# The last pass of an attention kernel: the order and the place of its sixteen late output projections

## The chip, the cores and the metric

The kernel runs on one core of a Trainium2 chip. The metric is the device time of one execution in microseconds (us). Before the change it is 1885.85 us, the median of three runs (1885.11 to 1886.77). PE is the matrix engine, DVE the vector engine, ACT the scalar engine, POOL the GpSimd engine; SP issues all the transfers spoken of here.

## The reference, cut to what matters

```
x  = L0_attn_x                     # (4, 2048, 256) fp32
xn = layernorm(x)
q, k, v = low-rank projections of xn, 16 heads of 16; rotary embedding on half of q and k
att = softmax(causal(q @ k^T / 4))
y   = (att @ v), heads side by side, (4, 2048, 256)
out = x + y @ Wc + feed_forward(xn)
```

The change concerns `y @ Wc` for the last of the four batches, and the addition of it to the residual `x + feed_forward(xn)`.

## The kernel before, in words

A first stage (up to about 490 us of the span) makes the weights, Q, K, V and the residual R = x + feed_forward(xn), and stores them in DRAM. The second stage is attention. Its work is cut into 16 passes, called quads: 4 batches by 4 groups of 4 heads. The code is unrolled over them (`quads`, L1241). A pass has three strands, which share PE:

- **Entries** (115 a pass, `NE`): PE fills one of 3 PSUM banks `sm` (`fill`, L1693), DVE reads it. Most entries are the row maxima of the scores that the next pass needs. In the passes 4 to 15, four of them are projections of the batch before (`project`, L1670): 128 rows of `y` times `Wc`, two blocks of 128 contraction rows (`a`), each an fp32 128x256 product, which the profile shows as two matmuls; `add` on DVE (L1568) adds the bank to the residual. Entry e can be filled only when entry e-3 has been read (L1694).
- **Scores** (68 units a pass): PE fills one of 2 PSUM banks `st` (L1725), ACT takes the exponential into one of 8 `prob` buffers (L1529).
- **Sums** (36 steps a pass, `STEPS`): PE multiplies the exponentials by V and gathers 512 columns in `pv` (L1738). Steps 0 to 2 belong to chunk 0 of the batch, 3 to 9 to chunk 1, 10 to 20 to chunk 2, 21 to 35 to chunk 3 (`STEP_AT` = 0, 3, 10, 21). After a chunk's last step ACT copies `pv` to `Y` (`evac`, L1508). On the diagonal steps (18 to 20 and 33 to 35 among them) POOL first masks the exponentials (L1488).

PE and ACT run the same hand-written order (`TIMETABLE`, L1044, turned into `PLANS`). The last pass has no next pass, so its plan, `LAST` (L1090), drops the next pass's entries from step 13 on. In their place stand one entry for the last row maxima (`ROWS_LAST`, just ahead of step 14) and sixteen **late projections**, those of the last batch, chunks 12 to 15 with 4 blocks each. `BEHIND` (L1078) says behind which step of the sums each of them stands. Engines work through their queues in order: an entry that can't start holds up everything behind it on PE.

What a late projection needs:

- The sums of a pass are moved by SP to DRAM and to `Yc` (`move`, L1281), reloaded, inverted on DVE (`invert`), stored, and spread over partitions (`spread_inverse`, L1301); then POOL multiplies `Yc` by them (`normalise`, L1443, `normalise_late`, L1449) and raises `normed`. Of quad 15, chunks 12 and 13 come as the first half (its `normalise` stands ahead of POOL's masks for step 33, at n = 23), and chunk 14 by itself (`move_third`, `invert_third`, `normalise_late(1)`, at n = 33).
- Chunk 15 of the last head group is done in the tail, after the last step (`TURNED` and behind, L1792). What its late projections do is the *other* 12 heads: `project(..., others=True)`, where the second block has 64 contraction rows in place of 128. They need only the sums of quad 14 (`normalise_late(0)`, at n = 25).
- `add` waits for the residual of the chunk: `r_loaded >= 16 * g + 16` (L1575), and r_loaded counts the loads in the order of the chunks. Chunk 12's residual is loaded in the pass before. Those of chunks 13, 14 and 15 are loaded in SP's queue of the last pass (L1369 to L1372), behind the moves of the first half, the maxima's loads, the inverse's store and spread, and `store_out(11)`; chunk 13's load waits for that store to have landed, since it reuses its buffer:

```
1369  if quad >= TC:
1370      store_out(quad - TC)
1371      for g in range(quad - TC + 2, NCH if last else quad - TC + 3):
1372          load_r(g)
```

Order of the late projections before: behind steps 24 to 29 two each (chunk 12, chunk 13, chunk 15's other heads, four each), behind steps 29 to 32 one each (chunk 14); so three stand behind step 29. DVE runs `invert` for chunk 14's sums after the fourth of them. What follows step 32 is the same in both kernels: the sums of steps 33 to 35, the copy, two rounds of transposes, the last head group's projection, the last add and store.

Of the kernel before, what the change touches and what calls it, by code (L numbers as in the profile page):

```python
# [18 lines left out]
NCH = B * T // CH  # L19
SUB = CH // P  # L20
TC = T // CH
G = 4
NQ = B * H // G
QB = H // G
# [965 lines left out]
NE = len(SEQ)  # L990
# [10 lines left out]
def half_of(e):  # L1001

    return SEQ[e][1][0][0] % 2
# [9 lines left out]
LAG = 3  # L1013
# [21 lines left out]
UNITS, STEPS = len(UNIT), len(STEP)  # L1035
STEP_OF = [max(n for n in range(STEPS) if any(u == v for _, _, src in STEP[n][1] for v, _ in src)) for u in range(UNITS)]
UNITS_OF = [sorted({u for _, _, src in STEP[n][1] for u, _ in src}) for n in range(STEPS)]
STEP_AT = [min(n for n in range(STEPS) if STEP[n][0] == c) for c in range(TC)] + [STEPS]
# [34 lines left out]

ROWS_LAST, FIRST_TWO, LAST_BEFORE, THIRD = NE, NE + 1, NE + 1 + 2 * SUB, NE + 1 + 3 * SUB
TURNED, TURNED_BACK, LAST_OWN = NE + 1 + 4 * SUB, NE + 2 + 4 * SUB, NE + 3 + 4 * SUB
BEHIND = {STEP_AT[TC - 1] + 3 + i: (FIRST_TWO + 2 * i, FIRST_TWO + 2 * i + 1) for i in range(6)}  # L1078
for i in range(SUB):
    n = STEPS - LAG - SUB + i  # L1080
    BEHIND[n] = BEHIND.get(n, ()) + (THIRD + i,)


def late_block(e):

    n, s = divmod(e - FIRST_TWO, SUB)
    return NCH - TC + (0, 1, 3, 2)[n], s


LAST = []  # L1090
for x in FULL:
# [4 lines left out]
    if x[0] == "sums" and x[1] == 0:  # L1096
        LAST += [("entry", 0, e) for e in BEHIND.get(x[2], ())]
PLANS = [FULL, LAST]
# [34 lines left out]
def attention(nc, io, w, scr):  # L1133

    with ExitStack() as ctx:
# [3 lines left out]
        def sem(name):  # L1139
            return ctx.enter_context(nc.semaphore(name))  # L1140
# [48 lines left out]
        inverse_spread = sem("inverse_spread")  # L1189
# [30 lines left out]
        def unit_done(quad, number):  # L1220
            return quad * UNITS_RUN + (XAHEAD + number + 1 + ST)

        def normed_for(g):

            return QB * (g // TC) + QB - 1 + g % TC // 2 + (g == NCH - 2)

        def residual(g):

# [176 lines left out]
        def _(pool):  # L1405
# [37 lines left out]
            def normalise(quad, half):  # L1443

                pool.wait_ge(inverse_spread, 16 * G * (2 * quad + half + 1))
                y = Yc[quad // QB % 2][:, quad % QB // 2, WIDE * half:WIDE * (half + 1)]
                pool.tensor_tensor(out=y, in0=y, in1=spread[half][:, :], op=ALU.mult).then_inc(normed, 1)

            def normalise_late(n):  # L1449

                y = Yc[(NQ - 1) // QB % 2][:, (NQ - 1) % QB // 2, WIDE:2 * WIDE]
                if n == 0:
                    pool.wait_ge(inverse_spread, 16 * G * (2 * NQ - 1))
                    pool.tensor_tensor(out=y[0:G * DH, CH:], in0=y[0:G * DH, CH:], in1=spread[1][0:G * DH, CH:], op=ALU.mult)\
                        .then_inc(normed, 1)
                else:
                    pool.wait_ge(normed, NQ)
                    pool.wait_ge(inverse_spread, 16 * G * 2 * NQ)
                    pool.tensor_tensor(out=y[:, 0:CH], in0=y[:, 0:CH], in1=spread[1][:, 0:CH], op=ALU.mult).then_inc(normed, 1)
# [8 lines left out]

            def body(quad, slot, last):
                for n in range(STEPS):  # L1470
                    if last and n == STEP_AT[TC - 1] + SUB:
                        normalise_late(0)
                    if last and n == STEP_AT[TC - 1] + SUB * (TC - 1):
                        normalise_late(1)
                    if n == STEP_AT[TC - 1] and quad and quad % 2 == 0:
                        normalise(quad - 1, 1)
                    if n == STEP_AT[TC - 1] + (2 if last else SUB + 2) and quad % 2:
                        normalise(quad, 0)
                    if n == STEP_AT[TC - 1] and not last:
                        place_v(quad + 1, (slot + 1) % SLOTS)  # L1480
                    if n == STEP_AT[TC - 1] and quad + 2 < NQ:
                        difference_of_keys(quad + 2, (quad + 2) % SLOTS, ((quad + 2) // SLOTS + 1) * (16 * LOADS))
                    if not DIAGONAL[n]:
                        continue
                    for u in UNITS_OF[n]:
                        wait_apart(pool, spare, exp_done, unit_done(quad, NUMBERS[last][u]), pool_steps, 1)
                        for x, count in diagonal_blocks(quad, n, u):
                            pool.affine_select(out=x, in_=x, compare_op=ALU.is_ge, fill=0.0, base=0,  # L1488
                                               pattern=[[0, count], [1, P]], channel_multiplier=-1).then_inc(masked, 1)
# [53 lines left out]
        def _(dve):  # L1543
# [86 lines left out]
            def body(quad, slot, last):  # L1630
                for e in range(AHEAD, NE):
                    take(quad, slot, e, last)
                    if e == INVERT_LATE and quad:
                        invert(2 * quad - 1)
                if last:
                    split_rows(quad, slot, ROWS_LAST, NG - 1, NG)
                    invert(2 * quad)
                    for e in range(FIRST_TWO, TURNED):
                        add(quad, slot, e, *late_block(e))
                        if e == FIRST_TWO + SUB - 1:  # L1640
                            invert(2 * quad + 1)
                    return
                for e in range(AHEAD):
                    if e == INVERT_EARLY:
                        invert(2 * quad)
                    take(quad + 1, (slot + 1) % SLOTS, e, quad + 1 == NQ - 1)

            quads(body)
            quad, slot, g = NQ - 1, (NQ - 1) % SLOTS, NCH - 1
# [5 lines left out]
            for s in range(SUB):  # L1655
                own = yn[:, s, G * DH:].rearrange("p (h k) -> p h k", h=G)
                i = dve.tensor_tensor(out=own, in0=turned[:, s, :, 0:DH], in1=rec[:, s, :, None].to_broadcast([P, G, DH]), op=ALU.mult)
# [11 lines left out]
        def _(pe):  # L1669
            def project(dst, g, s, others=False):  # L1670

                pe.wait_ge(wc_loaded, 16)
                if g < 0:
                    for a in range(CC):
                        i = pe.matmul(dst[:, 0:C], lhsT=w["ident"][:, :], rhs=Wc[:, a, :], start=a == 0, stop=a == CC - 1)  # L1675
                    i.then_inc(sm_ready, 1)
                    return
                pe.wait_ge(normed, normed_for(g))
                t = CH * (g % TC) + P * s
                for a in range(CC):  # L1680
                    r = slice(0, G * DH if others and a == CC - 1 else P)
                    i = pe.matmul(dst[:, 0:C], lhsT=Yc[g // TC % 2][r, a, t:t + P], rhs=Wc[r, a, :], start=a == 0, stop=a == CC - 1)  # L1682
                i.then_inc(sm_ready, 1)
# [9 lines left out]
            def fill(quad, slot, e):  # L1693
                pe.wait_ge(sm_read, quad * NE + e + 1)  # L1694
                dst = sm[(slot * NE + e) % SM]
                if e > NE or e < NE and SEQ[e][0] == "project":
                    g, s = (quad - TC, SEQ[e][1]) if e < NE else late_block(e)
                    project(dst, g, s, e >= LAST_BEFORE and e < THIRD)
                    return
                if e == NE or SEQ[e][0] == "rows":  # L1700
                    n = NG - 1 if e == NE else SEQ[e][1]
                    if e == NE or n < NG - 1:
                        pe.wait_ge(m_ready, quad * NG + n + 1)
                    elif quad:
                        pe.wait_ge(m_ready, quad * NG)
                    pe.transpose(dst[:, 0:P], m[:, :], w["ident"][:, :]).then_inc(sm_ready, 1)
                    return
                half["last"] = half_of(e)
                for h, t, k, at in SEQ[e][1]:
                    r, width = slice(ROW * (h % 2), ROW * (h % 2) + KD), block_width(t, k)  # L1710
                    i = pe.matmul(dst[:, at:at + width], lhsT=Q[slot][r, h // 2, t * P:(t + 1) * P],  # L1711
                                  rhs=K[slot][r, h // 2, k * CH:k * CH + width], start=True, stop=True)
                i.then_inc(sm_ready, 1)
# [78 lines left out]
            dst = late_bank(TURNED)  # L1792
            pe.wait_ge(pv_read, NQ * TC + 1)
            for s in range(SUB):
                t = (TC - 1) * CH + s * P
                i = pe.transpose(dst[:, s * P:(s + 1) * P], Y[:, t:t + P], w["ident"][:, :])
            i.then_inc(sm_ready, 1)
            dst = late_bank(TURNED_BACK)
            for s in range(SUB):
                pe.wait_ge(yn_ready, s + 1)  # L1800
                i = pe.transpose(dst[:, s * P:(s + 1) * P], yn[:, s, :], w["ident"][:, :])
            i.then_inc(sm_ready, 1)
            pe.wait_ge(sm_read, quad * NE + SM + TURNED_BACK + 1)
            for k in range(2):
                dst = late_bank(LAST_OWN + k)
                for a in range(2):
                    s = 2 * k + a
                    i = pe.matmul(dst[:, a * C:(a + 1) * C], lhsT=ynT[:, s * P:(s + 1) * P], rhs=Wc[:, CC - 1, :], start=True, stop=True)
# [75 lines left out]
```

## Time and profile before

| | |
|---|---|
| median of the runs | 1885.85 us |
| the profiled execution | 1885.63 us |
| its span | 1883.9 us |
| granted TensorE clock, mean over the span | 0.982 |
| busy, share of the span | PE 97%, DVE 89%, ACT 84%, POOL 28% |

The profile is of one execution, whose own time is 1.7 us above its span. All places below are in microseconds from the start of the span. The last pass's part with which this document deals lies between 1822 and 1884. In a timeline, a row gives start, duration, engine, line and operation, out<-in, and how many instructions are merged in it; in brackets how long the engine had been idle, and what released it.

### The profile page before, as it was taken

To read this page: it belongs to the slowest core of one execution; us is meant where nothing else is said; L and a number is where in the kernel's file an instruction comes from. 1 tells how busy PE (TensorE), PEld (TensorE's weight loads), DVE (VectorE), ACT (ScalarE), POOL (GpSimd) and SP (SyncE) were. 2 spreads that over 40 slices of the span, in tenths; PEclk is the share of its full clock that TensorE was granted. 3 is DMA by queue.
4 is the path that set the end of the run, shared out by engine and by line. 5 is a ranking of instruction groups with operands and counts; after the bars stand their busy time and mean duration, and the time that the engine had idled before them with its cause. 6 is when DMAs were issued, how large, how long until landed. Compare 5 with 4: busy or idle time off the path is not lost.

```text
span 1883.9 us, 41858 instructions
## 1 busy us (share of the span) xinstructions
PE 1820.1 (97%) x13875; PEld 681.7 (36%) x13875; DVE 1670.1 (89%) x4759; ACT 1591.1 (84%) x1924; POOL 536.8 (28%) x647
## 2 busy tenths in 40 slices
PE   6999999999789999999999999999999999999998
PEld 3556555555322323233232323323232322323223
DVE  5899999999789999999999999999999999999961
ACT  4676676675169999999999999999999999999994
POOL 1121121121244141523414152441415144141220
PEclk8999999999769999999999999999999999999999
DMA  5232333335422314041431414143141414324112
GB/s 185 68 106 84 90 104 89 89 100 123 103 63 46 58 24 65 22 73 25 78 54 49 65 45 84 32 83 53 50 65 45 79 35 84 53 50 65 36 36 81
DMA packets 160324, 129.01 MB, mean 68 GB/s; under 512 B 95344, under 2 KB 144752, under 8 KB 159768
## 3 DMA queue, kind: packets, MB, share of 16 engines
q1 hardware_dynamic: 159064, 126.84, 31.2%
q8 instruction: 89, 1.46, 0.3%
q14 instruction: 83, 0.68, 0.1%
q10 hardware_dynamic: 1088, 0.03, 0.0%
HBM read 74.60 MB, written 42.98 MB: 62 GB/s over the span
## 4 chain that ended last, share of the span: by engine, by line
PE 43%; ACT 15%; issue 8%; DVE 5%; DMA 1%; POOL 1%; SPq 1%; DVEq 0%; ACTq 0%; POOLq 0%
PE pv L1749 16%; ACT prob L1529 13%; PE sm L1711 10%; PE st L1734 10%; PE sm L1682 3%; PE st L1721 2%; DVE sm L1610 2%; ACT excess L1522 1%; DVE sm L1598 1%; PE sm L1675 1%; DVE pm L1615 1%; DMA scratch_i<-inverse 1%; DVE pm L1598 1%; DVE pm L1610 1%; ACT Y L1512 0%
## 5 line engine op out<-in xcount | busy, mean ns | idle before, releaser
L1529 ACT ACTIVATE prob<-st 128x1024 f32<-128x1024 f32 x1088 | 1048.1, 1028 | 53.6 <-PE st L1734 43.6
L1749 PE MATMUL pv<-prob,V 128*32 128x512 f32 (+3 forms) x5120 | 586.4, 539 | 0.3 <-ACT Y L1512 0.2
L1598 DVE CUSTOM_DVE_ANT_0 sm<-sm,mask 128x256 f32<-128x256 f32 (+3 forms) x1024 | 473.4, 520 | 32.0 <-PE sm L1711 27.3
L1711 PE MATMUL sm<-K,Q 48*128 48x512 f16 (+3 forms) x2112 | 479.7, 348 | 13.2 <-DVE pm L1598 5.5
L1734 PE MATMUL st<-Q,K 50*128 50x512 f16 (+3 forms) x2560 | 478.5, 352 | 9.8 <-ACT prob L1529 6.0
L1615 DVE TENSOR_REDUCE pm<-sm 128x1 f32<-128x512 f32 x640 | 412.0, 683 | 39.9 <-PE sm L1711 36.6
L1488 POOL TENSOR_SCALAR_AFFINE_SELECT prob<-prob 128x256 f32<-128x256 f32 (+1 forms) x448 | 191.4, 442 | 869.6 <-ACT prob L1529 860.5
L1610 DVE CUSTOM_DVE_ANT_0 sm<-sm,excess 128x512 f32<-128x512 f32 x448 | 301.2, 711 | 17.9 <-PE sm L1711 17.3
L1711 PEld LDWEIGHTS sm<-K,Q 48*128 48x128 f16 x2112 | 151.9, 95 | 327.9 <-DVE pm L1610 115.0
L1734 PEld LDWEIGHTS st<-Q,K 50*128 50x128 f16 x2560 | 125.7, 93 | 363.1 <-ACT prob L1529 265.2
L1522 ACT ACTIVATE excess<-st 128x1024 f32<-128x1024 f32 x218 | 220.4, 1024 | 8.7 <-DVE pm L1615 5.1
L1749 PEld LDWEIGHTS pv<-prob,V 128*32 128x32 f32 x5120 | 107.4, 108 | 172.8 <-issue 152.6
L1598 DVE DVE_READ_ACCUMULATOR2_ANT pm<- 128x1 f32 x1024 | 143.5, 140 | 0.1
L831 ACT ACTIVATE g<-bank 128x512 f32<-128x512 f32 x128 | 76.7, 599 | 55.8 <-PE bank L904 55.8
L722 DVE SCALAR_TENSOR_TENSOR gl<-g,wlnw,gh 128x512 f16<-128x512 f32 x128 | 106.9, 873 | 10.0 <-ACT gh L834 9.4
L866 PE MATMUL bank<-wWP,gh 128*128 128x256 f16 x512 | 113.6, 273 | 0.0
L866 PE MATMUL bank<-wWP,gl 128*128 128x256 f16 x512 | 113.5, 273 | 0.0
L1721 PE MATMUL st<-DK,Q 48*128 48x512 f16 x448 | 97.9, 389 | 7.1 <-POOL DK L1441 5.9
L659 POOL TENSOR_TENSOR frs<-fve,wmhalf 128x4 f32<-128x4 f32 x16 | 16.2, 1009 | 286.6 <-DVE fve L789 286.6
L834 ACT ACTIVATE gh<-g,wlnw 128x512 f16<-128x512 f32 x128 | 93.6, 731 | 0.0
L836 ACT ACTIVATE g<-g 128x512 f32<-128x512 f32 x128 | 81.5, 637 | 0.0
L904 PE MATMUL bank<-wxh,wWF 128*128 128x512 f16 x256 | 77.9, 386 | 0.1
(201 smaller groups left out, 1899.4 us busy)
## 6 DMA issues: line engine op xcount, KB each, us to landing
Q<-scratch_q SPq DMA_DIRECT2D x102, 128.0 KB, 4.3
K<-scratch_k SPq DMA_DIRECT2D x102, 128.0 KB, 7.1
x<-in_x SPq DMA_DIRECT2D x16, 512.0 KB, 4.4
scratch_v<-Rt SPq DMA_DIRECT2D x64, 128.0 KB, 2.0
scratch_r<-Rt SPq DMA_DIRECT2D x16, 512.0 KB, 3.2
V_raw<-scratch_v SPq DMA_DIRECT2D x16, 512.0 KB, 10.1
Yc<-Y SPq DMA_DIRECT2D x124, 64.0 KB
spread<-scratch_i SPq DMA_DIRECT2D x124, 64.0 KB, 2.2
```

The lines of the kernel that those rows point to most:

```text
L722: dve.scalar_tensor_tensor(out=gl[:, hc, :], in0=g[:, hc, 0, :], scalar=w["lnw"][:, hc:hc + 1], in1=gh[:, hc, :], op0=ALU.mult, op1=ALU.su ...
L866: pe.matmul(bank[s][:, 0:C], lhsT=x[:, hc, s * P:(s + 1) * P], rhs=w["WP"][:, hc, :], start=hc + k == 0, stop=hc + k == HC)
L1488: pool.affine_select(out=x, in_=x, compare_op=ALU.is_ge, fill=0.0, base=0, pattern=[[0, count], [1, P]], channel_multiplier=-1).then_inc(m ...
L1522: act.activation(excess[((slot + ahead) % SLOTS * NX + k) % EXCESSES][:, :, :], st[number % ST][:, :, :], ACT.Relu)\
L1529: act.activation(prob_of(quad, k)[:, :, :], st[number % ST][:, :, :], ACT.Exp).then_inc(exp_done, 1)
L1598: i = dve.tensor_tensor_reduce(x, x, mask[:, CH - block_width(t, k):], 1.0, -3e38, ALU.add, ALU.max, best(h, t, k))
L1610: dve.tensor_tensor_reduce(bank[:, :], bank[:, :], excess[(slot * NX + r) % EXCESSES][:, h % 2, :], 1.0, -3e38, ALU.add, ALU.max, best(h, ...
L1615: dve.tensor_reduce(out=best(h, t, k), in_=bank[:, :], axis=AX.X, op=ALU.max).then_inc(sm_read, 1)
L1711: i = pe.matmul(dst[:, at:at + width], lhsT=Q[slot][r, h // 2, t * P:(t + 1) * P], rhs=K[slot][r, h // 2, k * CH:k * CH + width], start=Tr ...
L1721: i = pe.matmul(st[number % ST][:, g, :], lhsT=Q[slot][rows[g], h // 2, t * P:(t + 1) * P], rhs=DK[slot][rows[g], h // 2, :], start=True, ...
L1734: i = pe.matmul(st[number % ST][:, a, at:at + width], lhsT=K[slot][r, hp, j * P:(j + 1) * P], rhs=Q[slot][r, hp, (c + 1) * CH - width:(c + ...
L1749: i = pe.matmul(pv[2 * DH * h:2 * DH * (h + 1), CH - width:CH], lhsT=V[quad % VSLOTS][:, j, h, :], rhs=prob_of(quad, u)[:, h % 2, at:at + ...
```

## The change

The late projections get another order (chunk 15's other heads first, then chunks 12, 13 and 14) and other places: behind steps 16, 18, 20 and 21; behind 21, 22, 23, 24; behind 25 to 28; behind 29 to 32. Only step 21 has two. On POOL `normalise_late(0)` moves from n = 25 to n = 10 and waits for the spread of quad 14 alone, and the counts of `normed` follow. DVE inverts chunk 14's sums after the sixth late entry in place of the fourth. The loads on SP stay as they are.

```diff
@@ -1073,18 +1073,16 @@
-ROWS_LAST, FIRST_TWO, LAST_BEFORE, THIRD = NE, NE + 1, NE + 1 + 2 * SUB, NE + 1 + 3 * SUB
+ROWS_LAST, LAST_BEFORE, FIRST_TWO, THIRD = NE, NE + 1, NE + 1 + SUB, NE + 1 + 3 * SUB
 TURNED, TURNED_BACK, LAST_OWN = NE + 1 + 4 * SUB, NE + 2 + 4 * SUB, NE + 3 + 4 * SUB
-BEHIND = {STEP_AT[TC - 1] + 3 + i: (FIRST_TWO + 2 * i, FIRST_TWO + 2 * i + 1) for i in range(6)}
-for i in range(SUB):
-    n = STEPS - LAG - SUB + i
-    BEHIND[n] = BEHIND.get(n, ()) + (THIRD + i,)
+LATE_AT = (16, 18, 20, 21) + (21, 22, 23, 24, 25, 26, 27, 28) + (29, 30, 31, 32)
+BEHIND = {n: [LAST_BEFORE + i for i, at in enumerate(LATE_AT) if at == n] for n in LATE_AT}
 
 def late_block(e):
-    n, s = divmod(e - FIRST_TWO, SUB)
-    return NCH - TC + (0, 1, 3, 2)[n], s
+    n, s = divmod(e - LAST_BEFORE, SUB)
+    return NCH - TC + (3, 0, 1, 2)[n], s
@@ -1222,7 +1220,9 @@
         def normed_for(g):
-            return QB * (g // TC) + QB - 1 + g % TC // 2 + (g == NCH - 2)
+            if g >= NCH - TC:
+                return NQ + (0, 0, 1, -1)[g % TC]
+            return QB * (g // TC) + QB - 1 + g % TC // 2
@@ -1450,7 +1450,7 @@
                 if n == 0:
-                    pool.wait_ge(inverse_spread, 16 * G * (2 * NQ - 1))
+                    pool.wait_ge(inverse_spread, 16 * G * (2 * NQ - 2))
@@ -1468,7 +1468,7 @@
                 for n in range(STEPS):
-                    if last and n == STEP_AT[TC - 1] + SUB:
+                    if last and n == STEP_AT[TC - 2]:
                         normalise_late(0)
@@ -1635,9 +1635,9 @@
                     invert(2 * quad)
-                    for e in range(FIRST_TWO, TURNED):
+                    for e in range(LAST_BEFORE, TURNED):
                         add(quad, slot, e, *late_block(e))
-                        if e == FIRST_TWO + SUB - 1:
+                        if e == FIRST_TWO + 1:
                             invert(2 * quad + 1)
@@ -1695,7 +1695,7 @@
-                    project(dst, g, s, e >= LAST_BEFORE and e < THIRD)
+                    project(dst, g, s, e >= LAST_BEFORE and e < FIRST_TWO)
```

## Rows read from the trace of the kernel before

**Rows 1.** Windows of the last pass: stretch, length, busy by engine, clock, DMA share, GB/s

```profile
1832.00:1837.00 5.00, 3.85 (x44) 1.19 (x42) 0.00 (x0) 4.90 (x7) 3.58 (x2) 1.00 0.54 164
1837.00:1842.00 5.00, 4.61 (x34) 0.93 (x34) 0.00 (x0) 4.97 (x6) 0.00 (x0) 1.00 0.92 297
...
1862.00:1867.00 5.00, 5.00 (x26) 2.22 (x24) 1.26 (x3) 1.93 (x2) 0.00 (x0) 1.00 0.01 3
```

**Rows 2.** Timeline of ACT, ahead of the late projections

```profile
1834.08 8.49 ACT L1529 ACTIVATE prob<-st 128x1024 f32<-128x1024 f32 x9
```

**Rows 3.** Timeline of PE: the sums of step 18 and of step 21

```profile
1830.05 1.06 PE L1749 MATMUL pv<-prob,V 128*32 128x512 f32 x8
...
1834.23 1.06 PE L1749 MATMUL pv<-prob,V 128*32 128x512 f32 x8 [0.18 <-ACT Y L1512]
```

**Rows 4.** Timeline of PE, 1854 to 1871: scores, and the sums of steps 28, 30, 31, 32

```profile
1854.40 0.61 PE L1734 MATMUL st<-Q,K 50*128 50x512 f16 x4
1855.97 0.39 PE L1734 MATMUL st<-Q,K 50*128 50x512 f16 x2 [0.96 <-ACT prob L1529]
1856.29 1.06 PE L1749 MATMUL pv<-prob,V 128*32 128x512 f32 x8
...
1865.12 1.07 PE L1749 MATMUL pv<-prob,V 128*32 128x512 f32 x8
...
1867.50 1.06 PE L1749 MATMUL pv<-prob,V 128*32 128x512 f32 x8
...
1870.10 1.06 PE L1749 MATMUL pv<-prob,V 128*32 128x512 f32 x8
```

**Rows 5.** The chain that ended last: two late projections (chunk 12, chunk 15), sums, one

```profile
1842.17 1.92 PE sm L1682 x8
...
1857.36 2.51 PE sm L1682 x8
...
1865.19 0.99 PE pv L1749 x8
1866.18 1.06 PE sm L1682 x4
```

**Rows 6.** Timeline of SP: a store, the residuals' loads, and the next move

```profile
1831.48 0.42 SPq L1344 DMA_DIRECT2D out<-Rt  x1
1834.53 0.40 SPq L1340 DMA_DIRECT2D Rt<-scratch_r  x1
1834.97 1.06 SPq L1340 DMA_DIRECT2D V<-scratch_r  x2
1836.07 1.24 SPq L1317 DMA_DIRECT2D scratch_l<-Y  x4
```

**Rows 7.** Line 1340 in the last pass: the residuals of chunks 13, 14, 15

```profile
DMA to landing us min/median/max: 4.0/5.0/6.5
```

**Rows 8.** Timeline of DVE: the first late add

```profile
1843.27 0.42 DVE L1576 TENSOR_TENSOR Rt<-Rt,sm 128x256 f32<-128x256 f32 x1 [19.88 <-PE sm L1682]
```

**Rows 9.** Timeline of POOL: normalising chunks 12 and 13, and chunk 14

```profile
1833.21 2.37 POOL L1447 TENSOR_TENSOR Yc<-Yc,spread 128x1024 f32<-128x1024 f32 x1 [2.77 <-DMA spread<-scratch_i]
...
1853.04 1.27 POOL L1459 TENSOR_TENSOR Yc<-Yc,spread 128x512 f32<-128x512 f32 x1 [16.25 <-DMA spread<-scratch_i]
```

**Rows 10.** Windows of PE alone at low clock: stretch, length, busy, clock, DMA share, GB/s

```profile
39.00:42.00 3.00, 1.82 (x3) 0.57 0.00 0
42.00:46.00 4.00, 3.94 (x11) 0.50 0.06 6
46.00:50.00 4.00, 4.00 (x19) 0.97 0.37 127
490.00:494.00 4.00, 0.00 (x0) 0.50 0.48 105
548.00:552.00 4.00, 4.00 (x38) 1.00 0.02 6
```

**Rows 11.** Timeline of PE: the first matmul of the attention stage

```profile
494.82 0.34 PE L1754 MATMUL pv<-ident 128*128 128x1 f32 x1 [6.17 <-PEq L539]
```

## The prediction

> **What bounds the kernel now.** I read the page's busy shares first (PE 97%), and then only the last pass, since nothing else is touched. Windows of five microseconds split that pass [rows 1]. Up to 1842 ACT is the full engine (4.90 and 4.97 of 5), and PE has gaps (3.85 and 4.61 busy): ACT takes nine exponentials without a pause [rows 2], and DVE, with nothing to do for 19.88 us, waits for the first late projection [rows 8]. From 1842 on the late projections sit on PE, which is then full while ACT falls to 1.93 of 5. So one part of the pass wastes PE and the next wastes ACT. What sets the end is PE's queue; the tail behind it is the same in both kernels. The most that an even spread can give back is PE's idle time ahead of 1842, of which these ten microseconds hold 1.54 (1.15 and 0.39), and a little from 1827 to 1832.
>
> **What the early places need.** Three conditions hold the first entries; I take them in turn.
> *Normalising.* Chunk 15's other heads need quad 14's sums only, a pass old, so POOL can multiply at n = 10. The nearest row, the same columns on twice the partitions, takes 1.27 us [rows 9]; I take that, and at nothing on the path, since POOL is busy for 28% of the span and its next work is the masks of step 18. If that cover were gone it would put those masks, and step 18, off by at most the 1.27. Chunk 12, now behind step 21, needs the multiply that starts at 1833.21 and takes 2.37, so it is ready at 1835.6 [rows 9].
> *Banks.* Of 3 `sm` banks one holds the last maxima, read long before. So the entries behind steps 16, 18 and 20 can be filled, and the fourth (the first behind step 21) waits until DVE has added the first.
> *The residual.* That first add is now chunk 15's, and waits for chunk 15's residual, where before it was chunk 12's, loaded a pass earlier. SP stores chunk 11 at 1831.48, waits for it, issues chunk 13's load at 1834.53 and the other two from 1834.97; the last is issued at about 1835.5 [rows 6]. Landing takes 4.0, 5.0 and 6.5 us [rows 7]; the queue is shared, so I give the longest to the last: 1835.5 + 6.5 = **1842.0**. Nothing that SP waits for ahead of it is moved by the change, so this time stays.
>
> **Where the stall is.** Before, step 21 starts at 1834.23 [rows 3] and its sums take 0.99 [rows 5], so the place of the fourth entry is reached at 1835.2. Three entries of chunk 15 now stand ahead of it: two of these took 2.51, so 1.25 each [rows 5], 3.8 in all. PE's waits for ACT take up part; if all, PE gets there at 1835.2, if none, at 1839.0. I take 1838, because ACT is already the slower engine there and only about 1 us of gaps lies between step 16 and step 21. PE then waits for the landing (1842.0), DVE's add (0.42 [rows 8]) and a hand-over of under 0.1: it goes on at **1842.5** after 4.5 us idle (3.5 to 7.3 by the bounds). Everything queued behind waits too: three score units, so ACT, which runs dry one exponential after the other, and step 22.
>
> **The sum, from 1842.5 to step 30.** Behind it PE is the bound to the end, so its pieces are added up at the prices of the rows.
> - The fourth entry, 1.25; the fifth, a full one, 1.06 [rows 5].
> - Three score units and then sums: 1854.40 to 1856.29 is 1.89, of which 0.96 is PE waiting for an exponential because there are 2 score banks [rows 4]. The same happens here.
> - A step of sums, one projection and two units takes 1870.10 - 1867.50 = 2.60 [rows 4]. From step 22 to step 27 there are five: 13.0.
> - Step 27 to 28 has three units: 0.99 + 1.06 + 1.89 = 3.94.
> - Step 28 to 29 has one unit: 1867.50 - 1865.12 = 2.38. Step 29 to 30: 2.60.
> Together 26.12, so step 30 starts at 1868.6. Before it starts at 1865.12 [rows 4]: **+3.5 us**. In this lies the dearer spread: two full ones together cost 1.92, alone 2.12, so four split pairs cost 0.8. From step 30 on both orders are the same, and nothing is added.
> What else moves costs nothing. Chunk 14's inverse is asked for after the sixth entry's add, about 1849.3, against 1847.9 before; its multiply was at 1853.04 [rows 9], so it comes at about 1854.5 and is wanted behind step 29, at 1866. The add itself (0.42 of DVE) is in time everywhere. `move_third` on SP needs chunk 2's copy, which comes some 2 us later (about 1836.3) than now but only 0.3 behind the queue's own 1836.07 [rows 6]. The stores of chunks 12 and 13 move to about 1854 and 1867, far from the last.
>
> **The clock.** A wait of 4.5 us does more than pass time. At 490 to 494 PE is idle and the granted clock is 0.50 [rows 10]; the first matmul after that ended 6.17 us of idleness [rows 11], so the fall to the 1.2 GHz level came within the first microseconds of it. Between 39 and 50 the clock is low for 0.43 / 0.5 of 3.00, all of 4.00 and 0.03 / 0.5 of 4.00, that is 2.6 + 4.0 + 0.2 = 6.8 us, and rises while PE works without a pause; the other stretch at the low level is the whole way from 490 to 548, on work full of short gaps [rows 10]. With no idle time like this in any pass of before, no row shows a gap of exactly this length. I price the fall by the nearest stretch, 6.8 us, since the work after the stall is dense: half of it is lost, 3.4, less about 0.4 because the 0.96 us wait for the exponential shrinks when PE is slow: **+3.0 us**. Bounds: 0 (no fall), and 26 / 2 = 13 if it stays low up to step 30.
> The Trainium skill, "TensorE: Matmul & The Clock Gate", section "HAM oscillation — how this bites in real kernels", describes just this: a wait for a transfer between bursts of matmuls sends the array back to half rate, and the next burst starts slow. By that rule the sum is 3.5 + 3.0; by a reading in which only the idle time counts it is 3.5.
>
> Sum: 1885.63 (the profiled execution's own time) + 6.5 = 1892.1. The median of the runs is 0.2 above that execution, so I forecast 1892.3.
>
> **The rivals.**
> A. *Stall and fallen clock*, as above: 1892.3. For it: the landing follows from SP's queue alone, and the clock's fall at 490. Chance 0.66.
> B. *Stall, and the clock holds.* The waits of up to 1 us in the last pass leave it at 1.00 [rows 1, 4]; 4.5 us might fall so that it holds too. 1885.85 + 3.5 = 1889.3. Chance 0.20; it straddles the bound of 0.2% (1889.6), so 0.13 of it is no change and 0.07 slower.
> C. *The clock stays low*, as it did from 490 to 548, because the steps' waits for ACT keep it there: 1885.85 + 3.5 + 13 = 1902. Against: PE leaves few gaps once it is the bound. Chance 0.05.
> D. *The residual is not late, and the gaps are filled.* Its place is the fourth entry; it decides if chunk 15's load has landed by 1838. Then PE goes on at 1838.0 (chunk 12's multiply, done at 1835.6, would be the next condition, and is met), and 1838.0 + 26.1 puts step 30 at 1864.1, 1.0 us earlier: 1884.8. With no ACT waits left at all it would be 1883; even that is within 0.2%. Against it: three loads of 512 KB behind a store, with DMA at 0.92 busy up to 1842 [rows 1]. Chance 0.09, of which 0.02 faster than 0.2%.
>
> **How the numbers follow.** 0.2% is 3.8 us, about what can be told from no change here. Slower: 0.66 + 0.07 + 0.05 = 0.78; same: 0.13 + 0.07 = 0.20; faster 0.02. The range starts at 1888.6, which takes in B, and ends at 1896.5, where the low stretch is about 14 us in place of 6.8. C and D are outside.
>
> **What would show it.** Right: in the new trace one idle time of PE of 4 to 5 us, ended by DVE's add to V (chunk 15's residual), ahead of the first of the two entries behind step 21; the first late add at about 1842.0, released by a DMA; ACT idle for some 6 us around 1839 to 1845; a granted clock below 1.00 in a window behind 1838; step 30 between 1868 and 1873; the tail unchanged in length. The step on the residual is wrong if the first late add starts well before 1841; the step on the clock if the windows keep 1.00. A time below 1885 would refute the argument as a whole.

## The result, and the profile after

| | before | changed |
|---|---|---|
| median | 1885.88 us (5 runs) | 1894.61 us (5 runs, 1893.09 to 1896.75) |
| ratio | | 1.0047, 95% interval 1.0036 to 1.0058 |
| profiled execution, span | 1885.63, 1883.9 | 1893.09, 1891.3 |
| mean granted clock | 0.982 | 0.980 |

The change costs 8.7 us. The ratios here and below leave out two executions of later rounds that ran far outside all others, one of the kernel before (5870 us) and one of the later start with its waits used (2012 us). The profiled execution of the changed kernel reached the last pass 1.1 us earlier than that of before (DVE splits the last maxima at 1821.74, and at 1822.85 before), a difference that stands already at the first sums of the attention (546.3, and 547.9 before), which the change doesn't touch. So 1.1 is to be added to its places before they are set against those of before; the span's 7.4 us more are 8.5 from there on.

PE's timeline of the changed kernel, from the sums of step 19 to step 30 (columns as in [rows 4]):

```profile
1832.78 1.50 PE L1749 MATMUL pv<-prob,V 128*32 128x384 f32 x24
...
1835.90 1.06 PE L1749 MATMUL pv<-prob,V 128*32 128x512 f32 x8
1841.35 4.38 PE L1682 MATMUL sm<-Wc,Yc 128*128 128x256 f32 x8 [4.38 <-DVE V L1576]
1845.65 1.03 PE L1734 MATMUL st<-Q,K 50*128 50x512 f16 x4
1847.44 0.61 PE L1734 MATMUL st<-Q,K 50*128 50x512 f16 x2 [0.75 <-ACT prob L1529]
1847.98 1.93 PE L1749 MATMUL pv<-prob,V 128*32 128x512 f32 x8
1849.84 2.08 PE L1682 MATMUL sm<-Wc,Yc 128*128 128x256 f32 x4
1851.85 1.03 PE L1734 MATMUL st<-Q,K 50*128 50x512 f16 x4
1852.82 1.51 PE L1749 MATMUL pv<-prob,V 128*32 128x512 f32 x8
1854.25 1.13 PE L1682 MATMUL sm<-Wc,Yc 128*128 128x256 f32 x4
...
1872.56 1.07 PE L1749 MATMUL pv<-prob,V 128*32 128x512 f32 x8
```

Two things are to be seen. PE is idle for 4.38 us behind step 21, and DVE's add to `V` (where chunk 15's residual lies) lets it go on. And for the next 12 us its work takes nearly twice as long: sums 1.93 for 1.06, one projection 2.08 for 1.13 (in [rows 4, 5], as after 1854 here, they have their old durations).

DVE's and ACT's timelines of the same stretch say who waits for what, and SP's and its landing when the data came:

```profile
1840.87 1.08 DVE L1576 TENSOR_TENSOR V<-V,sm 128x256 f32<-128x256 f32 x3 [18.59 <-DMA V<-scratch_r]
...
1852.30 0.35 DVE L1566 RECIPROCAL inverse<-sums 128x32 f32<-128x32 f32 x1
```

```profile
1846.36 2.85 ACT L1529 ACTIVATE prob<-st 128x1024 f32<-128x1024 f32 x3 [8.57 <-PE st L1734]
```

```profile
1833.89 1.06 SPq L1340 DMA_DIRECT2D V<-scratch_r  x2
```

```profile
DMA to landing us min/median/max: 4.0/5.0/6.3
```

The first late add was released by PE before [rows 8]; now a transfer releases it, and three adds follow at once, since three banks stood full. SP's loads are where they were [rows 6, 7], but for the 1.1 us. ACT stands for 8.57 us.

Windows of the changed kernel over the stall and behind it (columns as in [rows 1]):

```profile
1836.00:1840.00 4.00, 0.97 (x8) 0.06 (x8) 0.00 (x0) 1.80 (x2) 0.00 (x0) 1.00 1.07 356
1840.00:1844.00 4.00, 2.65 (x5) 1.35 (x6) 1.33 (x4) 0.00 (x0) 0.00 (x0) 0.51 0.05 7
1844.00:1848.00 4.00, 3.25 (x13) 1.08 (x13) 0.60 (x2) 1.64 (x2) 0.00 (x0) 0.50 0.00 0
1848.00:1852.00 4.00, 4.00 (x16) 1.49 (x16) 0.04 (x1) 1.22 (x2) 0.00 (x0) 0.50 0.01 4
1852.00:1856.00 4.00, 4.00 (x24) 1.14 (x24) 1.06 (x3) 2.13 (x3) 0.00 (x0) 0.78 0.09 21
1856.00:1860.00 4.00, 4.00 (x27) 1.47 (x22) 0.42 (x1) 3.34 (x4) 1.27 (x1) 1.00 0.23 64
```

The granted clock is at the 1.2 GHz level for 3.9 + 4.0 + 4.0 + 1.8 = 13.7 us, from just after 1840, while PE still stood, to about 1853.8.

**Where the 8.5 us are.** PE goes on at 1841.35 and starts step 30 at 1872.56: 31.2 us, where the prediction's pieces sum to 26.1 at full clock. So 5.1 us are the clock's, and 3.4 the stall's and the split pairs'. Of the 13.7 us at the low level 1.2 passed while PE still stood and cost nothing; over the other 12.4 the loss is 0.4 of the time, not half, since the work took 1.8 times as long (1.93 for 1.06) and the wait for an exponential was shorter. Behind step 30 the two traces run alike: from there to the tail's first transposes it is 10.83 us in both (1865.12 to 1875.95, and 1872.56 to 1883.39).

### The profile page after: what moved, and what is told of

It reads as the page before. It is cut to its first block, busy times and chain, and to the rows that moved or that the text cites. A ratio compares the mean times of both kernels' runs of the same rounds, so it can differ in the third digit from the quotient of the medians.

```text
span 1891.3 us, 41858 instructions
## 1 busy us (share of the span) xinstructions
PE 1826.5 (97%) x13875; PEld 685.3 (36%) x13875; DVE 1670.7 (88%) x4759; ACT 1591.4 (84%) x1924; POOL 535.9 (28%) x647
## 4 chain that ended last, share of the span: by engine, by line
PE 46%; ACT 12%; issue 7%; DVE 5%; DMA 2%; SPq 1%; POOL 1%; DVEq 0%; ACTq 0%; POOLq 0%
PE pv L1749 18%; PE st L1734 11%; PE sm L1711 11%; ACT prob L1529 10%; PE sm L1682 3%; PE st L1721 2%; DVE sm L1610 2%; DVE sm L1598 1%; ACT excess L1522 1%; PE sm L1675 1%; DVE pm L1615 1%; DMA scratch_i<-inverse 1%; DVE pm L1598 1%; DVE pm L1610 1%; PE sm L1706 0%
## 5 line engine op out<-in xcount | busy, mean ns | idle before, releaser
L1682 PE MATMUL sm<-Wc,Yc 128*128 128x256 f32 (+1 forms) x256 | 76.0, 420 | 4.8 <-DVE V L1576 4.4
```

## The experiments

Theory 1 is the prediction's: chunk 15's residual lands late, the fourth late entry waits, and the wait brings the clock down. Theory 2: the order or the spread costs by itself. Theory 3: chunk 12's multiply is the next thing to be late. Ratios are against the kernel before, on the same chip and in the same rounds (its medians there: 1885.90, 1886.42 and 1886.25 us). Each row stands for 3 to 11 executions, of which one has a profile.

| run | median us | ratio, 95% interval |
|---|---|---|
| early residual | 1884.81 | 0.9995 (0.9986 to 1.0004) |
| before, with the early load | 1886.38 | 1.0002 (0.9992 to 1.0011) |
| first of the three loads | 1887.46 | 1.0007 (0.9997 to 1.0016) |
| later start | 1884.26 | 0.9994 (0.9985 to 1.0003) |
| order alone | 1886.04 | 0.9997 (0.9988 to 1.0006) |
| stall filled, 20 matmuls | 1890.19 | 1.0023 (1.0013 to 1.0032) |
| stall filled, 15 | 1894.04 | 1.0039 (1.0027 to 1.0051) |
| stall filled, 10 | 1894.55 | 1.0041 (1.0026 to 1.0057) |
| changed kernel again | 1894.92 | 1.0045 (1.0030 to 1.0060) |
| before, two waits used | 1884.43 | 0.9989 (0.9980 to 0.9998) |
| early residual, waits used | 1883.27 | 0.9983 (0.9974 to 0.9992) |
| later start, waits used | 1883.85 | 0.9990 (0.9981 to 0.9999) |

### Taking the wait away: an earlier load

```diff
                     spread_inverse(quad - 1, 1)
+                if last:
+                    load_r(NCH - 1)
                 move(quad, 0)
...
-                    for g in range(quad - TC + 2, NCH if last else quad - TC + 3):
+                    for g in range(quad - TC + 2, NCH - 1 if last else quad - TC + 3):
```

Chunk 15's load and its add get a semaphore of their own, `last_loaded`.

> The changed kernel, but chunk 15's residual is loaded earlier in SP's queue, with a semaphore of its own. Theory 1 (the residual's late landing makes the stall, and the stall makes the clock fall): no PE idle time above 1 us in the last pass, clock 1.00 throughout, 1884.9 us, within 1 us. Theory 2 (the order itself costs: split pairs, fewer gaps, the clock falling on denser mixed work): the time stays above 1889. Theory 3 (chunk 12's multiply becomes the next wait): PE stalls some 1 to 2 us ahead of the fifth late entry, 1886 to 1887.

Measured: 1884.81 us. PE's timeline around the place of the stall:

```profile
1835.68 1.06 PE L1755 MATMUL pv<-prob,V 128*32 128x512 f32 x8
1836.67 2.39 PE L1688 MATMUL sm<-Wc,Yc 128*128 128x256 f32 x8
1838.99 0.61 PE L1740 MATMUL st<-Q,K 50*128 50x512 f16 x4
1840.57 0.39 PE L1740 MATMUL st<-Q,K 50*128 50x512 f16 x2 [0.96 <-ACT prob L1532]
...
1862.78 1.06 PE L1755 MATMUL pv<-prob,V 128*32 128x512 f32 x8
```

Step 21's sums go straight over into the fourth and fifth entries; the longest wait is the known 0.96 for an exponential. From the fourth entry to step 30 it is 26.1 us, and the granted clock is 1.00 in all of 1830 to 1880. The whole loss is gone with one load, so neither the order nor the spread nor chunk 12's multiply makes it. The control, on the kernel before:

> Control: the kernel before with the same earlier load of chunk 15's residual. No theory has a gain for it, since no add of before waits for a residual: 1885.9 us, within 0.7 us. If it gained, the gain of the first run would be the load's and not the order's.

1886.38 us, no gain: the load matters only where something waits for it.

### A dose of the landing

```diff
+                    if last:
+                        sp.wait_ge(out_stored, 16 * (NCH - TC))
+                        load_r(NCH - 1)
-                    for g in range(quad - TC + 2, NCH if last else quad - TC + 3):
+                    for g in range(quad - TC + 2, NCH - 1 if last else quad - TC + 3):
```

> The changed kernel, but chunk 15's residual is the first of the three loads behind the store, not the last; nothing else of the queue moves. It is issued at about 1834.5 and lands after 4.0 us, at 1838.5, the add is done at 1838.95: PE waits about 1 us in place of 4.4. Theory 1: the stall follows the landing; 1884.8 + 1.0 = 1885.8 us if the clock holds as in the waits of 0.96, some 4 more if it falls. Were the wait for anything but the landing, it would stay at 4.4 us.

PE's, then DVE's timeline of it:

```profile
1838.02 2.38 PE L1689 MATMUL sm<-Wc,Yc 128*128 128x256 f32 x8 [1.04 <-DVE V L1583]
```

```profile
1837.54 1.08 DVE L1583 TENSOR_TENSOR V<-V,sm 128x256 f32<-128x256 f32 x3 [15.25 <-DMA V<-scratch_r]
```

The wait follows the landing: 1.04 us in this execution. The profiled execution took 1884.63 us with the clock at 1.00; the median, 1887.46, is 1.7 above what I expected. The ten executions spread from 1884.63 to 1889.74, and only one has a profile. That in some of them the clock fell would fit, but isn't shown.

### The place and the order apart

```diff
-LATE_AT = (16, 18, 20, 21) + (21, 22, 23, 24, 25, 26, 27, 28) + (29, 30, 31, 32)
+LATE_AT = (18, 20, 22, 23) + (24, 24, 25, 25, 26, 26, 27, 28) + (29, 30, 31, 32)
```

> The changed kernel with chunk 15's four entries behind steps 18, 20, 22 and 23, then two behind each of 24, 25 and 26, and one behind each of 27 to 32; the loads are untouched. Theory 1: the fourth entry is reached at about 1841.7, the wait for the residual shrinks to under 1 us, the clock holds, and PE's gaps up to 1842 are partly filled: 1884.9 us, within 1 us. Theory 2 (order): most of the loss stays, above 1889.

1884.26 us: the four entries stand two steps later (and six of the other twelve in pairs again), and the loss is gone without touching a load. DVE's first add waits for the transfer as in the changed kernel, but PE has work until then. DVE's, then PE's timeline of it, up to the fourth entry:

```profile
1841.75 1.08 DVE L1576 TENSOR_TENSOR V<-V,sm 128x256 f32<-128x256 f32 x3 [18.69 <-DMA V<-scratch_r]
```

```profile
1841.40 1.06 PE L1749 MATMUL pv<-prob,V 128*32 128x512 f32 x8
1842.40 1.11 PE L1682 MATMUL sm<-Wc,Yc 128*128 128x256 f32 x3
```

With the order alone, all in the old places (24, 24, 25, 25, and so on):

> The changed kernel's order (chunk 15's other heads first, then 12, 13, 14) in the places of before: two behind each of steps 24 to 28, three behind 29, one each behind 30 to 32. Theory 1 (only the place against the landing of the residual matters): the first add comes after 1843, when the residual is there, so nothing waits: 1885.9 us, within 0.7. Theory 2 (the order costs by itself): above 1887.

1886.04 us. The order costs nothing, and gains nothing.

### The clock apart from the stall

The stall's length is fixed by the landing, so work put into it doesn't prolong it while it ends by then; it only keeps PE busy. (The twenty matmuls below end just with it: DVE's first add starts at 1841.26 and PE goes on at 1841.74.)

```diff
+            def keep_busy(quad, slot, count):
+                number = XAHEAD + NUMBERS[True][45]
+                pe.wait_ge(exp_done, quad * UNITS_RUN + number + 1)
+                for _ in range(count):
+                    pe.matmul(st[number % ST][:, 0, :], lhsT=K[slot][0:KD + 2, 0, 0:P], rhs=Q[slot][0:KD + 2, 0, 0:CH],
+                              start=True, stop=True)
```

It is called ahead of the fourth late entry.

> The changed kernel with 20 matmuls of 128x512 put in ahead of the fourth late entry, into a score bank that is overwritten next; their results are not used. They fill the stall with work and remove nothing of it. Theory 1: PE still goes on only when the residual has landed (about 4.4 us lost to filler), but the clock stays at 1.00, so only the stall's part is left: 1885.9 + 3.5 = 1889.4 us, and the difference to the changed kernel, about 5 us, is the clock's price. Theory 2 (the clock falls for another reason, or costs little): the time stays at 1894 or is above it.

PE's timeline:

```profile
1836.26 1.07 PE L1756 MATMUL pv<-prob,V 128*32 128x512 f32 x8
1837.30 4.49 PE L1742 MATMUL st<-Q,K 50*128 50x512 f16 x20
1841.74 2.39 PE L1682 MATMUL sm<-Wc,Yc 128*128 128x256 f32 x8
...
1867.84 1.06 PE L1756 MATMUL pv<-prob,V 128*32 128x512 f32 x8
```

and its windows:

```profile
1836.00:1842.00 6.00, 6.00 (x31) 2.22 (x30) 0.74 (x3) 1.94 (x2) 0.00 (x0) 1.00 0.80 255
1842.00:1850.00 8.00, 7.03 (x40) 2.76 (x40) 1.87 (x6) 4.36 (x5) 0.00 (x0) 1.00 0.03 4
```

With 4.4 us of useless work added and nothing removed the kernel is 4.4 us *faster* than the changed one (1890.19 against 1894.61). The clock stays at 1.00, and from the fourth entry to step 30 it takes 1867.84 - 1841.74 = 26.10 us. This splits the loss by medians: 4.3 us for the stall and the pairs (1890.19 - 1885.90; 3.5 were expected), 4.4 for the clock. One of the ten executions took 1894.11; it has no profile.

Ten and fifteen of the matmuls in place of twenty:

> As the kernel with 20 filler matmuls, but with 10: about 2.2 us of the stall stay idle. The stall's length is the same, so only the clock can differ. If a wait of this length brings the clock down as 4.4 us did: about 1894. If it does not: 1890, as with 20. I expect it to fall in some executions, with a median of 1891 and a wider spread than with 20.

> 15 filler matmuls in the stall, between 10 (2.12 us left idle, the clock fell) and 20 (0.0 idle, it held). About 1.1 us stay idle, as much as the waits of 0.96 which leave the clock at 1.00 everywhere. If the length of a single wait decides: the clock holds, 1890.2 us. If it falls here too, something else in that stretch (the filler's kind of work, the sparse steps ahead) is needed beside the wait: about 1894.

Ten leave 2.12 us idle, fifteen 0.98, as PE's timelines have it:

```profile
1843.45 4.37 PE L1682 MATMUL sm<-Wc,Yc 128*128 128x256 f32 x8 [2.12 <-DVE V L1576]
```

```profile
1841.57 2.39 PE L1682 MATMUL sm<-Wc,Yc 128*128 128x256 f32 x8 [0.98 <-DVE V L1576]
```

With ten, all four executions took 1893.24 to 1895.39 us, and the profiled one shows 4.37 us for two projections, the low level. I had expected 1891. Its windows have the fall within the wait:

```profile
1838.00:1842.00 4.00, 3.33 (x19) 0.98 (x18) 0.00 (x0) 1.86 (x2) 0.00 (x0) 1.00 1.08 352
1842.00:1846.00 4.00, 2.55 (x5) 1.25 (x6) 1.23 (x4) 0.00 (x0) 0.00 (x0) 0.58 0.07 11
```

PE stands from 1841.33, and by the 0.58 the low level begins at about 1842.6, 1.3 us later. In the changed kernel it began 3.1 us after PE fell idle (1836.97 to 1840.1). So a wait of 2.12 us behind ten filler matmuls is enough.

With fifteen, two of six took 1888.86 and 1889.80 and four 1893.55 to 1896.55. The 1889.80 is the profiled one: 2.39, full clock. The gap of 4 us between the two groups is that between the kernels with 20 and with 10, so I read it as the clock falling in four of six. That is read from times alone: in the one profile, with 0.98 us idle, the clock held, and how long PE waited in the four others isn't recorded. So it isn't shown that a wait of 0.98 us can bring the clock down. The waits of 0.96 behind steps 21 and 27 leave it at 1.00 in the traces of the early residual and of the kernels with 15 and 20. Whether the filler's narrow operands (50 rows) or the sparse steps ahead play a part was not tried. The Trainium skill, "TensorE: Matmul & The Clock Gate", section "HAM oscillation — how this bites in real kernels", tells of waits for transfers of several microseconds that bring the clock down; the changed kernel agrees with it, 4.38 us and then 13.7 at the low level. A fall in a wait of 2.12 us it does not tell of.

The changed kernel once more:

> The changed kernel once more, for a second look at its clock: the stall is 4.4 us again; the time at the low level may differ from 13.65 us, since the five runs of it spread over 3.7 us. 1894.6 us.

1894.92 us; windows of its profiled execution (1896.35 us):

```profile
1840.00:1844.00 4.00, 0.00 (x0) 0.00 (x0) 0.05 (x1) 0.57 (x1) 0.00 (x0) 1.00 0.81 248
1844.00:1848.00 4.00, 3.58 (x7) 2.10 (x8) 1.45 (x4) 0.00 (x0) 0.00 (x0) 0.51 0.02 2
1848.00:1852.00 4.00, 3.25 (x16) 0.52 (x15) 0.42 (x1) 2.56 (x3) 0.00 (x0) 0.50 0.01 4
1852.00:1856.00 4.00, 4.00 (x24) 1.45 (x16) 0.68 (x2) 1.16 (x2) 0.00 (x0) 0.71 0.00 0
```

Here the low level lasts 3.9 + 4.0 + 2.3 = 10.2 us in place of 13.7. It began 4.3 us after PE fell idle, and 3.1 us in the first profile; that is 1.2 of the 3.5 us, and what makes the rest isn't shown. Both profiles have the whole stall, 4.4 and 4.7 us. From the fourth entry to step 30 it takes 1874.49 - 1844.42 = 30.07 us, so the clock costs 4.0 us here and 5.1 in the first profile. The execution is the longer one all the same: the last maxima are split 2.8 us later (1824.51, for 1821.74), and the last projection runs at the low level.

### Using PE's waits

The gains so far are within the noise. Two waits of PE in the kernel before can be filled without any of the change: the 0.96 us behind step 27 [rows 4], and the one ahead of the last step's sums, which wait for the last unit's exponential and mask.

```diff
+for e, n, u in ((FIRST_TWO + 7, STEP_AT[TC - 1] + 6, 59), (THIRD + SUB - 1, STEPS - LAG - 1, 67)):
+    BEHIND[n] = tuple(k for k in BEHIND[n] if k != e)
+AMID = {59: (FIRST_TWO + 7,), 67: (THIRD + SUB - 1,)}
...
+    if x[0] == "scores":
+        LAST += [("entry", 0, e) for e in AMID.get(x[2], ())]
```

> The kernel before, with two of its late projections moved into PE's waits: the second of those behind step 27 goes between the second and the third score unit behind it (PE waits 0.96 there), and the last one goes behind the last score unit, so that its exponential and its mask run beside it (PE has some 0.6 idle ahead of the last step of sums). If PE is the bound to the end: 1885.9 - 1.5 = 1884.4 us. If the tail is bound elsewhere: 1885.9.

1884.43 us, 0.9989 (0.9980 to 0.9998): as expected, and with an interval below 1. The same with the early load, and with the later start (a string names the score unit behind which an entry stands):

```diff
+LATE_AT = (16, "39", 18, 20) + ("46", 22, 23, 24, 25, 26, 27, "59") + (28, 29, 31, "67")
...
+LATE_AT = (18, 20, "46", 23) + (23, 24, 24, 25, 25, 26, 27, "59") + (28, 29, 31, "67")
```

> The early load of the residual with the late projections from step 16 on, each put where PE waits: behind step 16, after the first unit behind 17, behind 18 and 20, after the second unit behind 21, behind 22 to 27, after the second unit behind 27, behind 28, 29 and 31, and after the last unit. Theory 1: no stall, clock 1.00, and against the early load alone (1884.8) the two waits of 0.96, half of one of 0.43 and the 0.6 ahead of the last step are filled: 1882.1 us. If PE's waits come back elsewhere: 1884 to 1885.

> No load is moved. Chunk 15's entries behind steps 18 and 20, after the second unit behind 21 and behind 23; the rest one or two a step, with one in the wait behind step 27 and one behind the last unit. Theory 1: the wait for the residual is under 1 us and the clock holds; against the kernel with the later start (1884.3) the wait of 0.96 and the 0.6 ahead of the last step go: 1882.8 us, as good as with the early load (1883.3).

1883.27 us (0.9983, 0.9974 to 0.9992) and 1883.85 us (0.9990, 0.9981 to 0.9999). Both beat both kernels; they can't be told from each other, nor clear of noise from the kernel before with its two waits used (1884.43). Against the kernel before of their own rounds they gain 3.2 and 2.4 us; of this the two waits give 2.0 by themselves (1886.42 - 1884.43), and the earlier places about 1, which is what the first experiment had given (1885.90 - 1884.81 = 1.1, itself within the noise). The first was expected at 1882.1 and came at 1883.27, the second at 1882.8 and came at 1883.85. PE's waits behind step 27 in the first are gone:

```profile
1855.44 0.60 PE L1743 MATMUL st<-Q,K 50*128 50x512 f16 x4
1855.97 1.13 PE L1691 MATMUL sm<-Wc,Yc 128*128 128x256 f32 x4
1857.04 0.39 PE L1743 MATMUL st<-Q,K 50*128 50x512 f16 x2
```

## Why the prediction was right, and where it was off

- **The residual, not the multiply or the bank count alone.** Right. The load was to land at 1842.0 and PE to go on at 1842.5; it went on at 1841.35, which with the 1.1 us of the earlier start is 1842.45. The idle time was to be 4.5 us and is 4.38. ACT was to be idle for some 6 us and stood for 8.57: the two projections behind the stall, which stand ahead of its next scores on PE, took 4.38 us in place of 2.39.
- **The sum from there to step 30.** Right: 26.12 was predicted, and both kernels in which the clock held show 26.1 (early residual, stall filled). That includes the dearer single projections.
- **What was taken at nothing.** POOL's multiply ran at n = 10 in POOL's idle time. Chunk 14's inverse came at 1852.30, which in the places of before is 1853.4, not 1849.3, because the low clock delayed the sixth entry, and its multiply at 1857.31; it was wanted behind step 29, at about 1871. The tail is unchanged.
- **The clock.** The mechanism was right: it fell within the stall. The term was mis-sized: 6.8 us at the low level and 3.0 us lost were predicted, 13.7 and 10.2 us were seen, 5.1 and 4.0 us lost in the two profiled executions. The size that was off is the length of the low stretch, and a likely reason lies in the row that I chose. The stretch of 6.8 us [rows 10] ended under work without a pause, and I called the work after the stall dense; but it holds the wait for an exponential behind step 21, 0.75 us at 1847.44, so that the window 1844 to 1848 has PE busy for 3.25 of 4.00. I had counted this wait in the sum and not in the clock. In both profiles of the changed kernel the clock rose only some microseconds behind it (6.3 and 3.8); that it is the cause was not tried by itself. With 5.1 in place of 3.0 the forecast is 1894.4, against 1894.61 measured; that the range still held the result is owed to its upper end, which was set for a low stretch of about 14 us.
- **A bound in the sum was too low.** If the clock had stayed low up to step 30, 26.1 us of work would have taken about twice as long, so the loss would be some 26 us, not 26 / 2 = 13. The halving is of time spent at the low level (6.8 us of it lose 3.4), and 26.1 us is the work at full clock. By the loss of 0.4 found above it would be some 17 us (43.5 us at the low level for that work). An estimate of rival C's time is so 1907 to 1915, not 1902.
- **The rivals.** B (the clock holds) is what the kernel with the stall filled shows: 1890.19, for 1889.3. D (the residual in time) is the kernel with the early load: 1884.81, for 1884.8. That it agrees to 0.01 us is luck, as executions of this kernel spread from 1883.30 to 1887.85. C did not occur.

## What to carry to other kernels

When an entry is moved earlier in a queue, every wait in front of its consumer moves with it: here POOL's multiply was moved along, and the load that DVE's add needs was not. Read from the trace when each input lands, and move the earliest place no further than that, or move the load. And where one engine must wait some microseconds for data in a stretch in which it is the bound, count the clock as well: it doubled the price of this stall.

## What the runs showed of the hardware that was not expected

- In the stretch of the stall, 2.12 us idle behind 10 small fp16 matmuls left all four executions as slow as 4.4 us idle did. With 15 four of six were as slow; the one with a profile, 0.98 us idle, was not. Filled to the end, nine of ten stayed at 1888.4 to 1891.4 us.
- The clock can fall in the tail, among transposes and short waits. In the profiled execution of the kernel with the later start and the waits used, the last projection runs at the low level:

```profile
1875.37 3.42 PE L1811 MATMUL sm<-Wc,ynT 128*128 128x256 f32 x8 [0.69 <-ACT ynT L1543]
```

  where ten of the fourteen profiled executions, that of before among them, have 1.99; the other four have 3.36 to 3.62. This alone moves an execution by 1.4 to 1.6 us, as much as the gains sought here, though the instructions are the same.
- Late projections with 64 contraction rows in the second block cost more, not less, when another projection follows: one of them and a full one take 2.32 us from start to the next unit (1836.67 to 1838.99, early residual), two full ones 1.93 (1842.10 to 1844.03, before). The 2.51 for two of them against 1.92 [rows 5] may hold a score matmul, which in the timeline of before starts at 1859.18, ahead of the last of the eight. When score units follow, hardly anything is left: from the projection to the next sums 1.69 us (1834.21 to 1835.90, changed kernel), and 1.60 with a full one (1854.25 to 1855.85). What makes the difference isn't shown.
